# A second cross attention with its scores made twice, in rows and in columns, a norm moved between engines, and another order at the program's end

## The chip, the cores and the metric

The kernel runs on one core of one Trainium2 chip. The metric is the device time of one execution of the whole program, in microseconds, as the median of several executions. Engines are named as in the profile: PE is TensorE, PEld its weight loads, DVE VectorE, ACT ScalarE, POOL GpSimd, SP the engine that issues DMAs.

## The reference, cut to what matters

A decoder of two layers works on x of shape (16, 112, 256), with a context of shape (16, 375, 256). Each layer is self attention, cross attention over the context and a feed-forward part, and each of the six ends in a layer norm over x plus its result. The change touches the second layer: the cross attention (16 heads of 16 dimensions), the norm behind the coupled self attention ahead of it, and the end of the last part.

```python
q = x @ W_q + b_q
kv = memory @ W_kv + b_kv
scores = jnp.einsum('bhqd,bhkd->bhqk', q, k) * (1.0 / np.sqrt(HD))
scores = jnp.where(pad[:, None, None, :], -jnp.inf, scores)
A = jax.nn.softmax(scores, axis=-1)
ctx = jnp.einsum('bhqk,bhkd->bhqd', A, v)
...
x = _layernorm(x + y @ W_o + b_o, axis=-1)
```

## The kernel before, in words

The program is a row of stages (`stage_...` functions). Inside a stage every engine runs its own hand-written list of work, and semaphores (`then_inc`, `wait_ge`) tie the lists together. No planner moves anything: the order on an engine is the order in the source, and an engine that waits holds up all that is behind it on that engine. The helper `split_product` (lines 102 to 106) writes one exact product as three, of high and low parts, so its matmuls carry the lines 104, 105 and 106 in every stage.

`stage_cross_attention` serves both layers; the second call (`cross1`) is the one replaced. It loops over the 16 batches, and in a batch over 16 heads, with the batch after it prepared in between ("front": the context turned, C0 and C1; queries, Q; keys, K0 and K1; values, V0 to V2). Queries and keys are split in high and low parts, stored to DRAM and loaded back stacked (`stack`, lines 592 and 597), so that one product of 96 rows makes an exact score. For a head i of a batch, PE makes the scores in rows, 112 queries by 376 keys (line 730), DVE adds the mask, copies them out of PSUM and takes the maximum in one instruction (line 941), ACT makes exponentials (line 845), PE turns the probabilities three blocks at a time so that the keys lie on partitions (`turn`, line 738), ACT and DVE in turns copy them back to SBUF (lines 851 and 948), and PE multiplies them with the values, four heads at a time (line 751). Tables in each engine's list say at which head a front unit or a part of the tail runs:

```python
TAIL_AT = {6: 0, 8: 1, 10: 2, 15: 3}
FRONT_AT = {2: V0, 4: V1, 6: V2, 7: C0, 8: C1, 10: Q, 12: K0, 14: K1}
```

`stage_coupled_attention`, the stage before it, loops over the same batches with four groups of four heads. Its norm is made by DVE (`normalise`, line 1428) from y, a mean and POOL's power (`root`, line 1106); ACT has a list with two pairs of `tanh` (lines 1299 and 1304), the copy of the heads' columns (`copy_columns`, line 1330) behind them, and copies of turned probabilities (line 1324).

`stage_switch` is the last stage. Behind its 128 slots, eight "units" of gated outputs are left. For each, DVE multiplies by gates (`by_gates`, line 2692), ACT rounds the product (`high`, line 2602), POOL makes the low part (`low`, line 2421), and PE does twelve products (`outputs`, lines 104 to 106). Sums, statistics and norms of four chunks of four batches each (lines 2703 to 2724) stand between them on DVE.

## Time and profile before

| | us |
|---|---|
| median of 3 runs (lowest, highest) | 2426.97 (2423.71, 2427.23) |
| the profiled execution, its own time | 2411.24 |
| its span in the trace | 2409.5 |
| PE busy (share) | 2186.7 (91%) |
| DVE busy | 1728.6 (72%) |
| ACT busy | 1275.1 (53%) |
| POOL busy | 535.0 (22%) |

The shares are averages over all stages. What a change in one stage is worth is read from that stage: from the period of its loop, from what PE waits for in it, and from the rows in order of time. The second cross attention takes the time from about 1145 to 1519 us of the span, the coupled attention that from about 937 to 1143, and the last stage that from about 1532 to the end.

### The profile page before, as it was taken

Reading aid. Unit: us, or ns where it says so; the run is one execution under the profiler, and the core shown is the slowest. Engines: PE = TensorE matmul, PEld = TensorE weight load, DVE = VectorE, ACT = ScalarE, POOL = GpSimd, SP = SyncE. Lnnn points to the kernel's source line nnn. Section 1 sums busy time; section 2 is a strip of 40 time slices with the busy share of each in tenths; the row PEclk is TensorE's granted clock in tenths of the full one; section 3 lists DMA queues with packets and bytes.
Section 4 is the critical chain, followed back from the end, with each engine's and each line's share of the span. In section 5 each row is a group of like instructions: output and inputs, shape, how many; then the busy total and the mean of one; then the engine's idle time right before and its main releaser. Section 6 shows DMA issues by size and latency. Waiting matters only on the chain. (4 is left out here: it accounts for less than half of the span.)

```text
span 2409.5 us, 48067 instructions
## 1 busy us (share of the span) xinstructions
PE 2186.7 (91%) x15771; PEld 1847.9 (77%) x15771; DVE 1728.6 (72%) x4277; ACT 1275.1 (53%) x2676; POOL 535.0 (22%) x435
## 2 busy tenths in 40 slices
PE   7789999868999987897899998799999999999995
PEld 5578777757999965664787887678888888888884
DVE  2467877775888864776577777677777777767564
ACT  3257666754666634665566666444444444444441
POOL 3200000041111062332100000023333333333333
PEclk9889999988999998999899999899999999999998
DMA  4066666323766521000666664133232333222222
GB/s 117 4 149 135 131 129 131 81 74 104 235 207 213 172 66 35 0 0 0 149 131 128 132 142 109 56 97 92 93 99 87 112 89 102 88 94 93 71 76 69
DMA packets 201755, 246.50 MB, mean 102 GB/s; under 512 B 58481, under 2 KB 176706, under 8 KB 201602
## 3 DMA queue, kind: packets, MB, share of 16 engines
q1 hardware_dynamic: 198050, 235.37, 37.2%
q0 software_dynamic: 3552, 9.18, 1.3%
q8 instruction: 85, 1.39, 0.2%
q14 instruction: 68, 0.56, 0.1%
HBM read 202.95 MB, written 41.55 MB: 101 GB/s over the span
## 5 line engine op out<-in xcount | busy, mean ns | idle before, releaser
L845 ACT ACTIVATE cross_pr<-cross_sc,cross_mn 112x375 f32<-112x375 f32 x512 | 307.4, 607 | 222.8 <-DVE cross_mn L941 221.9
L2421 POOL TENSOR_TENSOR switch_gl<-switch_gb,switch_gh 128x896 fp32r<-128x896 f32 x128 | 270.7, 2116 | 574.8 <-ACT switch_gh L2602 574.8
L941 DVE CUSTOM_DVE_ANT_0 cross_sc<-cross_ps,cross_masked 112x375 f32<-112x375 f32 x512 | 271.6, 544 | 83.3 <-PE cross_ps L730 81.2
L738 PE MATMUL cross_ps<-all_ident,cross_pr 112*125 112x112 f32 x1536 | 255.7, 275 | 42.8 <-DVE cross_pt L948 41.9
L738 PEld LDWEIGHTS cross_ps<-all_ident,cross_pr 112*125 112x125 f32 x1536 | 232.5, 189 | 68.1 <-DVE cross_pt L948 38.9
L2658 DVE SCALAR_TENSOR_TENSOR switch_vt<-switch_ps,switch_chosen,switch_vt 112x128 f32<-112x128 f32 x512 | 144.1, 345 | 191.7 <-PE switch_ps L106 186.9
L730 PE MATMUL cross_ps<-cross_k,cross_q 96*112 96x376 f32 x512 | 212.8, 416 | 13.4 <-DMA cross_k<-cross_k_dram 11.6
L104 PE MATMUL switch_ps<-switch_vw,switchgates_xh 128*112 128x512 f32 x512 | 209.2, 408 | 4.9 <-ACT switch_vt L2581 4.9
L104 PE MATMUL switch_ps<-switch_gh,switch_ow 128*128 128x448 f32 x512 | 192.5, 376 | 18.6 <-POOL switch_gl L2421 17.3
L106 PE MATMUL switch_ps<-switch_vw,switchgates_xl 128*112 128x512 f32 x512 | 202.3, 395 | 0.0
L105 PE MATMUL switch_ps<-switch_vw,switchgates_xh 128*112 128x512 f32 x512 | 201.6, 394 | 0.0
L2581 ACT ACTIVATE switch_vt<-switch_ps,switch_chosen 112x128 f32<-112x128 f32 x512 | 145.9, 367 | 93.5 <-PE switch_ps L106 80.7
L105 PE MATMUL switch_ps<-switch_gl,switch_ow 128*128 128x448 f32 x512 | 190.6, 372 | 0.0
L106 PE MATMUL switch_ps<-switch_gh,switch_ow 128*128 128x448 f32 x512 | 190.4, 372 | 0.0
L2602 ACT CAST switch_gh<-switch_gb 128x896 fp32r<-128x896 f32 x128 | 121.7, 951 | 52.5 <-DVE switch_gb L2692 51.7
L672 POOL TENSOR_TENSOR cross_rstd<-cross_var,cross_half 112x1 f32<-112x1 f32 x32 | 17.3, 541 | 580.0 <-DVE cross_var L963 580.0
L2692 DVE TENSOR_TENSOR switch_gb<-switch_gb,switch_ct 128x896 f32<-128x896 f32 x128 | 138.6, 1084 | 0.0
L104 PE MATMUL experts_ps<-experts_xh,experts_w 128*128 128x256 f32 (+1 forms) x400 | 124.7, 312 | 6.4 <-ACT experts_h L1929 3.0
L948 DVE COPY cross_pt<-cross_ps 125x336 f32<-125x336 f32 x256 | 128.3, 501 | 1.6 <-PE cross_ps L738 1.5
L104 PEld LDWEIGHTS switch_ps<-switch_gh,switch_ow 128*128 128x128 f32 x512 | 98.2, 192 | 38.2 <-POOL switch_gl L2421 20.0
L730 PEld LDWEIGHTS cross_ps<-cross_k,cross_q 96*112 96x112 f32 x512 | 90.7, 178 | 43.1 <-issue 27.7
L1929 ACT ACTIVATE experts_h<-experts_ps,experts_b1c 128x256 f32<-128x256 f32 x168 | 79.9, 475 | 81.5 <-PE experts_ps L106 79.2
(399 smaller groups left out, 5656.2 us busy)
## 6 DMA issues: line engine op xcount, KB each, us to landing
switch_gb<-switch_gt_rows SPq DMA_DIRECT2D x128, 448.0 KB, 3.6
experts_w_raw<-in_L_ffn_w_dram SPq DMA_DIRECT2D x42, 1024.0 KB, 5.4
cross_k<-cross_k_dram SPq DMA_DIRECT2D x96, 375.0 KB, 8.0
cross_k_dram<-cross_ks SPq DMA_DIRECT2D x32, 750.0 KB, 4.7
all_place<-in_ctx_dram SPq DMA_DIRECT2D x32, 375.0 KB
cross_q<-cross_q_dram SPq DMA_DIRECT2D x192, 56.0 KB, 4.5
all_place<-in_L_ffn_v_w_dram SPq DMA_DIRECT2D x16, 512.0 KB, 6.2
all_place<-in_L_ffn_o_w_dram SPq DMA_DIRECT2D x8, 1024.0 KB, 7.4
```

What stands on the lines that cost most here:

```text
L104: nc.tensor.matmul(out, w[0], x[0], start=first, stop=False)
L105: nc.tensor.matmul(out, w[0], x[1], start=False, stop=False)
L106: return nc.tensor.matmul(out, w[1], x[0], start=False, stop=last)
L730: nc.tensor.matmul(ps[0:T, SCORES + h % 2, 0:KEYS], q[parity][:, h // 2, h % 2, :], kk[parity][:, h // 2, :], start=True, stop=True).then_ ...
L738: last = nc.tensor.transpose(ps[0:KP, TURNED + h % 2, t * T:(t + 1) * T], pr[:, h % NB, t * KP:(t + 1) * KP], ident[0:T, 0:T])
L845: nc.scalar.activation(pr[:, h % NB, :], sc[:, h % NB, :], ACT.Exp, bias=mn[parity][:, h:h + 1], scale=-1.0).then_inc(exped, 1)
L941: nc.vector.tensor_tensor_reduce(out=sc[:, h % NB, :], in0=ps[0:T, SCORES + h % 2, 0:S2], in1=mask_of[:], scale=-0.25, scalar=3e38, op0=AL ...
L948: nc.vector.tensor_copy(pt[:, h % NB, :], ps[0:KP, TURNED + h % 2, 0:KT * T]).then_inc(pt_dve, 1)
L2421: pool.tensor_tensor(gl[u % 2][:], gb[u % RING][:], gh[u % 2][:].bitcast(F32), ALU.subtract)\
L2581: last = nc.scalar.activation(vt[b % 2][:, e, :], ps[0:T, VALUES, e * PW:(e + 1) * PW], ACT.Copy, scale=chosen[h % 2][:, b, e:e + 1])
L2658: last = nc.vector.scalar_tensor_tensor(out=part, in0=ps[0:T, VALUES + 1, e * PW:(e + 1) * PW], scalar=chosen[h % 2][:, b, EH + e:EH + e + ...
L2692: nc.vector.tensor_tensor(gb[u % RING][:], gb[u % RING][:], ct[n % 2][:].unsqueeze(1).broadcast_to([P, EU, CT]), ALU.mult).then_inc(gated, 1)
```

## The change

**Second cross attention** (`stage_cross_columns`, in the place of the second call of `stage_cross_attention`). The scores are made twice. PE makes them in rows, as before (97 stacked rows: the mask is now a row of the stacked keys, made by POOL), and DVE only takes the maximum. When the maxima of eight heads are there, PE turns them, DVE splits minus the maxima in a high and a low part (`split_maxima`), and SP copies these by one DMA for each head and part, 16 for a half batch, into two more rows of the stacked queries (`stack_maxima`). PE then makes the scores again in columns, keys on partitions, four heads and 125 keys at a time (`columns`: two products of 256 columns), now with mask and minus maximum inside, and ACT makes exponentials of 448 elements a partition, straight into the tile that PE multiplies with the values. Turning the probabilities and copying them back (lines 738, 851 and 948) falls away. Three of a batch's twelve column units run in its own loop step, nine in the next; the tail lags two batches. Stacks are loaded by halves.

```diff
+        MASK_ROW, MAX_ROW, ROWS = 3 * PAIR, 3 * PAIR + 1, 3 * PAIR + 3
...
+        Q_PARTS, K_PARTS, M_PARTS = 6, 3, H
+        COLUMNS_OF_LAST = {1: 3, 2: 4, 3: 5, 5: 6, 6: 7, 7: 8, 9: 9, 10: 10, 11: 11}
+        COLUMNS_AT = {13: 0, 14: 1, 15: 2}
+        VALUES_AT = {1: 0, 5: 1, 9: 2, 13: 3}
+        HALF_OF_LAST_AT, HALF_AT = 1, 9
...
+            def stack_maxima(b, parity, part):
+                wait_apart(sp, sp_passed, (m_ready, b * HALVES + part + 1))
+                for n, bits in enumerate((mh, ml)):
+                    for h in range(H // 2):
+                        sp.dma_start(q[parity][MAX_ROW + n:MAX_ROW + n + 1, part * 4 + h // 2, h % 2, 0:T].bitcast(F32),
+                                     bits[part][h:h + 1, :].bitcast(F32)).then_inc(m_stacked[part], 16)
...
+                nc.tensor.matmul(ps[0:T, SCORES + h % 2, 0:KEYS], q[parity][0:MAX_ROW, h // 2, h % 2, 0:T],
+                                 kk[parity][0:MAX_ROW, h // 2, :], start=True, stop=True).then_inc(s_done, 1)
...
+            def turn_maxima(b, parity, part):
+                pe.wait_ge(s_max, b * H + (part + 1) * (H // 2))
+                nc.tensor.transpose(ps[0:H // 2, SCORES + 1, TURNED_AT:TURNED_AT + T],
+                                    mx[parity][:, part * (H // 2):(part + 1) * (H // 2)], ident[0:T, 0:T]).then_inc(m_turned, 1)
+
+            def columns(b, parity, n):
+
+                g, t = n // KT, n % KT
+                if n % (UNITS_OF_COLUMNS // 2) == 0:
+                    pe.wait_ge(m_stacked[2 * n // UNITS_OF_COLUMNS], (b + 1) * M_PARTS * 16)
+                wait(pe, exped, b * UNITS_OF_COLUMNS + n - 1)
+                for i in range(2):
+                    pair = 2 * g + i
+                    last = nc.tensor.matmul(ps[0:KP, COLUMNS + n % 2, i * 2 * QCOLS:(i + 1) * 2 * QCOLS],
+                                            kk[parity][:, pair, t * KP:(t + 1) * KP],
+                                            q[parity][:, pair].rearrange("r i t -> r (i t)"), start=True, stop=True)
+                last.then_inc(st_done, 1)
...
+                nc.scalar.activation(pt[:, n % RING], ps[0:KP, COLUMNS + n % 2, :].rearrange("p (a b) -> p a b", b=QCOLS)[:, :, 0:T],
+                                     ACT.Exp, scale=0.25).then_inc(exped, 1)
...
+                nc.vector.reduce_max(mx[parity][:, h:h + 1], ps[0:T, SCORES + h % 2, 0:S2], axis=AX.X).then_inc(s_max, 1)
...
+            def split_maxima(b, part):
+
+                wait_apart(dve, dve_passed, (m_turned, b * HALVES + part + 1), (m_stacked[part], b * M_PARTS * 16))
+                bank = ps[0:H // 2, SCORES + 1, TURNED_AT:TURNED_AT + T]
+                nc.vector.tensor_scalar_mul(mh[part][:], bank, -1.0).then_inc(m_high, 1)
+                wait_apart(dve, dve_passed, (m_high, b * HALVES + part + 1))
+                nc.vector.scalar_tensor_tensor(out=ml[part][:], in0=bank, scalar=-1.0, in1=mh[part][:].bitcast(F32),
+                                               op0=ALU.mult, op1=ALU.subtract).then_inc(m_ready, 1)
```

On SP, a step of the loop of the second cross attention before is this (two batches make one turn of the loop; `cross1_q1` and `cross1_k1` are the stacked queries and keys of odd batches).

```order
L576 DMA cross1_q_dram1<-cross1_qs 128x4x112
...
L580 DMA cross1_k_dram1<-cross1_ks 128x4x375
...
L564 DMA all_place1<-in_ctx_1024_dram 125x3x256
...
L569 DMA cross1_mask_raw0<-in_mask_BxS2_bf1_dram 112x375
...
L592 DMA cross1_q1<-cross1_q_dram1 16x8x112 x6
L597 DMA cross1_k1<-cross1_k_dram1 32x8x375 x3
```

And this is one step of it in the changed kernel (`cross1_mh` and `cross1_ml` are the high and low parts of minus the maxima).

```order
L1158 DMA cross1_q1<-cross1_mh1 1x16x7 x8
L1158 DMA cross1_q1<-cross1_ml1 1x16x7 x8
...
L1146 DMA cross1_q1<-cross1_q_dram1 16x4x112 x6
L1150 DMA cross1_k1<-cross1_k_dram1 32x4x375 x3
...
L1116 DMA all_place1<-in_ctx_1024_dram 125x3x256
...
L1121 DMA cross1_mask_raw0<-in_mask_BxS2_bf1_dram 1x375
...
L1158 DMA cross1_q0<-cross1_mh0 1x16x7 x8
L1158 DMA cross1_q0<-cross1_ml0 1x16x7 x8
...
L1146 DMA cross1_q1<-cross1_q_dram1 16x4x112 x6
L1150 DMA cross1_k1<-cross1_k_dram1 32x4x375 x3
...
L1127 DMA cross1_q_dram0<-cross1_qs 128x4x112
...
L1131 DMA cross1_k_dram0<-cross1_ks 128x4x375
```

A step has grown from 13 DMAs to 54: 32 rows of maxima, and the 9 loads of a stack are now 18 of half the size, with each batch of 16 rows between them.

On PE, this is what the changed kernel has from the turning of a batch's first eight maxima (line 1304) to the first of the column units that need them (the last row; line 1299 is a score in rows, 1315 a column unit, 1328 values, 1276 queries).

```order
L1304 MATMUL cross_ps<-all_ident,cross_mx 8x112
...
L1315 MATMUL cross_ps<-cross_q,cross_k 125x256 x2
L1354 MATMUL cross_ps<-all_ident,cross_xn 128x112 x2
...
L1328 MATMUL cross_ps<-cross_pt,cross_v 32x112 x12
...
L1299 MATMUL cross_ps<-cross_k,cross_q 112x376
L1315 MATMUL cross_ps<-cross_q,cross_k 125x256 x2
...
L1276 MATMUL cross_ps<-all_xt,all_place 128x112 x3
...
L1299 MATMUL cross_ps<-cross_k,cross_q 112x376
...
L1315 MATMUL cross_ps<-cross_q,cross_k 125x256 x2
```

Between the turn and that unit stand, in all, two other column units, one turned norm, one quad of values, four scores, the queries and the first half of the keys.

**Norm of the coupled attention.** POOL also makes minus mean times the root, and ACT, not DVE, makes the normed rows, ahead of its copy of group 2; DVE makes minus the mean; ACT's copy of the columns goes ahead of the tanh.

```diff
                 if before:
+                    copy_columns(b - 1)
                 if not last:
                     tanh(b + 1, 1 - parity)
...
+                if before == 2:
+                    normalise(b - 2)
                 evacuate(b, 2)
...
+                nc.scalar.activation(xn[:], y[:], ACT.Identity, bias=offset[:], scale=rstd[:]).then_inc(xn_ready, 1)
...
+                nc.vector.tensor_scalar_mul(minus_mean[:], mv[:, 0:1], -1.0)
```

**End of the last stage.** For the last eight units POOL makes the low part of one expert and DVE that of the other, and DVE's list behind slot 128 is written out by hand.

```diff
+                experts = slice(0, EU if u < SHARED else EU // 2)
+                pool.tensor_tensor(gl[u % 2][:, experts, :], gb[u % RING][:, experts, :],
+                                   gh[u % 2][:, experts, :].bitcast(F32), ALU.subtract).then_inc(low_ready, 1)
...
+                nc.vector.tensor_sub(gl[u % 2][:, 1, :], gb[u % RING][:, 1, :], gh[u % 2][:, 1, :].bitcast(F32))\
+                    .then_inc(low_dve, 1)
```

On DVE, before, from the gates of the sixth of the eight units on (2692 gates, 2703 sum, 2710 to 2719 statistics, 2724 norm):

```order
L2692 TENSOR_TENSOR switch_gb<-switch_gb,switch_ct 128x896
L2710 TENSOR_TENSOR all_x<-all_x,switch_ps 112x1024
L2714 BN_STATS switch_st<-all_x 112x6 x4
L2717 BN_AGGR switch_mv<-switch_st 112x2 x4
L2719 TENSOR_SCALAR switch_var<-switch_mv 112x4
L2724 TENSOR_SCALAR all_x<-all_x,switch_mv,switch_rstd 112x256 x4
L2692 TENSOR_TENSOR switch_gb<-switch_gb,switch_ct 128x896 x2
L2703 TENSOR_TENSOR switch_yt<-switch_ps,switch_yt 128x2x448
```

and in the changed kernel, from the gates of the seventh on (3273 gates, 3354 low part, 3284 sum, 3291 to 3300 statistics, 3305 norm):

```order
L3273 TENSOR_TENSOR switch_gb<-switch_gb,switch_ct 128x896
L3305 TENSOR_SCALAR all_x<-all_x,switch_mv,switch_rstd 112x256 x4
L3273 TENSOR_TENSOR switch_gb<-switch_gb,switch_ct 128x896
L3354 TENSOR_TENSOR switch_gl<-switch_gb,switch_gh 128x448
L3291 TENSOR_TENSOR all_x<-all_x,switch_ps 112x1024
L3295 BN_STATS switch_st<-all_x 112x6 x4
L3298 BN_AGGR switch_mv<-switch_st 112x2 x4
L3300 TENSOR_SCALAR switch_var<-switch_mv 112x4
L3354 TENSOR_TENSOR switch_gl<-switch_gb,switch_gh 128x448
```

The gates of the last two units now stand ahead of the statistics of the third chunk, not behind them.

## Rows read from the trace of the kernel before

**Rows 1.** Busy time by stretch: second cross attention's loop, then the program's end.
```profile
1168.80:1508.50 339.70, 315.47 (x3320) 271.89 (x3320) 269.48 (x888) 232.43 (x510) 21.29 (x44) 0.99 0.62 131
2346.00:2403.60 57.60, 33.30 (x147) 28.28 (x146) 32.85 (x73) 9.05 (x11) 22.11 (x12) 0.85 0.21 66
```
(Columns: stretch, its length, busy time of PE, PEld, DVE, ACT and POOL with counts, granted clock, DMA share, GB/s.)

**Rows 2.** PE in order of time, one batch: start, length, what, idle before.
```profile
1300.47 0.33 PE L730 MATMUL cross_ps<-cross_k,cross_q 96*112 96x376 f32 x1
1300.64 0.48 PE L738 MATMUL cross_ps<-all_ident,cross_pr 112*125 112x112 f32 x3
1300.88 0.41 PE L730 MATMUL cross_ps<-cross_k,cross_q 96*112 96x376 f32 x1
...
1301.38 0.36 PE L104 MATMUL cross_ps<-cross_w_high,cross_cx_high 128*125 128x256 f32 x1
...
1302.26 0.78 PE L751 MATMUL cross_ps<-cross_pt,cross_v 125*32 125x112 f32 x24
...
1309.13 1.06 PE L713 MATMUL cross_ps<-all_xt,all_place 128*128 x8
1310.20 1.12 PE L770 MATMUL cross_ps<-all_place,cross_o 128*112 128x256 f32 x4
1310.97 0.52 PE L730 MATMUL cross_ps<-cross_k,cross_q 96*112 96x376 f32 x1
...
1312.07 0.42 PE L104 MATMUL cross_ps<-cross_cx_high,cross_w_high 128*128 128x376 f32 x1
...
1313.28 0.78 PE L751 MATMUL cross_ps<-cross_pt,cross_v 125*32 125x112 f32 x24
1313.99 0.42 PE L730 MATMUL cross_ps<-cross_k,cross_q 96*112 96x376 f32 x1
1315.04 0.58 PE L738 MATMUL cross_ps<-all_ident,cross_pr 112*125 112x112 f32 x3 [0.63 <-DVE cross_pt L948]
...
1322.42 0.33 PE L730 MATMUL cross_ps<-cross_k,cross_q 96*112 96x376 f32 x1
```

**Rows 3.** Groups of PE instructions, 1200 to 1450 us: busy, mean ns, idle before.
```profile
L738 PE MATMUL cross_ps<-all_ident,cross_pr 112*125 112x112 f32 x543 | 90.3, 275 | 16.2 <-DVE cross_pt L948 16.2
```

**Rows 4.** Groups of DVE instructions, the same stretch.
```profile
L941 DVE CUSTOM_DVE_ANT_0 cross_sc<-cross_ps,cross_masked 112x375 f32<-112x375 f32 x182 | 96.6, 544 | 25.3 <-PE cross_ps L730 24.5
L926 DVE SCALAR_TENSOR_TENSOR cross_qs<-cross_ps,all_qk_bias,cross_qs 128x112 fp32r<-128x112 f32 x24 | 6.9, 328 | 0.0
```

**Rows 5.** SP in order of time: DMA issues (start, length for all xN).
```profile
493.71 0.25 SPq L1642 DMA_DIRECT2D experts_b_all<-in_L_ffn_bs_dram  x1
...
907.72 7.29 SPq L1080 DMA_DIRECT2D coupled_Jd<-in_L_attn_J_attn_dram  x16
...
1301.22 2.85 SPq L592 DMA_DIRECT2D cross_q<-cross_q_dram  x6
```

**Rows 6.** The page's list of DMA issues: KB each, median us to landing.
```profile
coupled_Jd<-in_L_attn_J_attn_dram SPq DMA_DIRECT2D x16, 1.0 KB, 1.5
```

**Rows 7.** PE alone by stretches of 3 us: busy, granted clock, DMA share, GB/s.
```profile
2349.00:2352.00 3.00, 0.51 (x3) 1.00 0.00 0
2352.00:2355.00 3.00, 3.00 (x11) 0.57 0.41 158
...
2361.00:2364.00 3.00, 0.21 (x2) 1.00 0.00 0
2364.00:2367.00 3.00, 2.74 (x12) 1.00 0.41 149
```

**Rows 8.** Coupled attention, all engines in order of time, one batch.
```profile
1061.63 0.53 ACT L1330 COPY coupled_osb<-coupled_ps 128x448 f32<-128x448 f32 x1
...
1062.21 0.65 PE L1208 MATMUL coupled_ps<-all_ident,coupled_osb 128*112 128x128 f32 x4 [1.29 <-ACT coupled_osb L1330]
...
1063.08 1.75 DVE L1428 TENSOR_SCALAR coupled_xn<-coupled_y,coupled_mv,coupled_rstd 112x256 f32<-112x256 f32 x1 [0.62 <-POOL coupled_rstd L1106]
```

**Rows 9.** The program's end, all engines in order of time.
```profile
2378.66 1.22 DVE L2710 TENSOR_TENSOR all_x<-all_x,switch_ps 112x1024 f32<-112x1024 f32 x1 [2.73 <-PE switch_ps L2528]
...
2383.14 2.09 DVE L2692 TENSOR_TENSOR switch_gb<-switch_gb,switch_ct 128x896 f32<-128x896 f32 x2
...
2385.27 4.13 POOL L2421 TENSOR_TENSOR switch_gl<-switch_gb,switch_gh 128x896 fp32r<-128x896 f32 x2 [2.01 <-ACT switch_gh L2602]
```

More of the change, by code:

```diff
@@ L1105, in root @@
                 pool.wait_ge(var_ready, b + 1)
-                pool.tensor_tensor(rstd[:], var[:], half[:], ALU.pow).then_inc(rstd_ready, 1)
+                pool.tensor_tensor(rstd[:], var[:], half[:], ALU.pow).then_inc(root_ready, 1)
+                pool.wait_ge(root_ready, b + 1)
+                pool.tensor_tensor(offset[:], minus_mean[:], rstd[:], ALU.mult).then_inc(rstd_ready, 1)
             def store(b):
@@ L1334, in copy_output, with normalise @@
                 nc.scalar.copy(o[:].rearrange("p a b -> p (a b)"), ps[:, TAIL, 0:DC * T]).then_inc(o_ready, 1)
+            def normalise(b):
+                act.wait_ge(rstd_ready, b + 1)
+                wait(act, x_stored, b)
+                nc.scalar.activation(xn[:], y[:], ACT.Identity, bias=offset[:], scale=rstd[:]).then_inc(xn_ready, 1)
             def copy_normed(b):
@@ L1349, in batch @@
                 exponent(b, 1)
+                if before:
+                    copy_columns(b - 1)
                 if not last:
                     tanh(b + 1, 1 - parity)
-                if before:
-                    copy_columns(b - 1)
                 evacuate(b, 1)
@@ L1358, in batch @@
                     turned_tanh(b + 1, 1 - parity)
+                if before == 2:
+                    normalise(b - 2)
                 evacuate(b, 2)
@@ L1417, in statistics @@
             def statistics(b, ch):
+                wait(dve, xn_ready, b)
                 ch.link(nc.vector.tensor_add(y[:].unsqueeze(1), x[:, ds(b, 1), :], o_bias[:].unsqueeze(1)))
@@ L1440, in batch @@
                 shift(b, 2, ch)
-                if before == 2:
-                    normalise(b - 2)
                 if before:
@@ L2386, in load_gates @@
                 wait(sp, low_ready, u - RING + 1)
+                wait(sp, low_dve, u - RING + 1 - SHARED)
                 sp.dma_start(gb[u % RING][:].rearrange("p e s -> p (e s)"),
@@ L2432, in _ @@
                     low(u)
-                c = turned_at(g)
-                if c is not None:
+                for c in ROOTS_BEHIND.get(u, ()):
                     root(c)
@@ L2505, in outputs @@
                 pe.wait_ge(low_ready, u + 1)
+                wait(pe, low_dve, u + 1 - SHARED)
                 if i == 0:
@@ L2736, in _ @@
             steps = iter(())
-            for g in range(END):
+            for g in range(SLOTS):
                 p, b = g // B, g % B
@@ L2767, in _, with low @@
                         nc.vector.tensor_sub(low_bits, raw, high_bits.bitcast(F32)).then_inc(ow_low, 1)
-                c = turned_at(g)
-                if c is not None:
-                    statistics(c)
-                    if c:
-                        normalise(c - 1)
-            normalise(NC - 1)
+            def low(u):
+                dve.wait_ge(high_ready, u + 1)
+                wait(dve, unit_done, u - 1)
+                nc.vector.tensor_sub(gl[u % 2][:, 1, :], gb[u % RING][:, 1, :], gh[u % 2][:, 1, :].bitcast(F32))\
+                    .then_inc(low_dve, 1)
+            last, u = HS * NC - 1, SHARED
+            attend(last, 0)
+            by_gates(u)
+            add_columns(last - 2)
+            by_gates(u + 1)
+            low(u)
+            attend(last, 1)
+            by_gates(u + 2)
+            low(u + 1)
+            statistics(0)
+            by_gates(u + 3)
+            low(u + 2)
+            low(u + 3)
+            statistics(1)
+            by_gates(u + 4)
+            low(u + 4)
+            by_gates(u + 5)
+            add_columns(last - 1)
+            low(u + 5)
+            by_gates(u + 6)
+            normalise(0)
+            by_gates(u + 7)
+            low(u + 6)
+            statistics(2)
+            low(u + 7)
+            normalise(1)
+            add_columns(last)
+            statistics(3)
+            normalise(2)
+            normalise(3)
 def stage_store(nc, x, out):
```

481 lines of the change are left out of this document (469 added, 12 removed).

## The prediction

> **What bounds the kernel now.** I read the busy time by stretch first. In the loop of the second cross attention PE is busy 315.47 of 339.7 us, DVE 269.48 and ACT 232.43 [rows 1]: PE sets the pace, DVE and ACT have some 20 to 30% to spare. The rows in order of time then show what PE does. From one batch's score at 1300.47 to the same one at 1322.42 is a period of 21.95 us, and starts are close behind each other, with one wait of 0.63 us for DVE's copy of turned probabilities at 1315.04 [rows 2]. The groups say how much of that there is: 16.2 us in 250 us before line 738 [rows 3], or 1.4 us in each of the 11.4 batches that such a stretch holds. What counts is therefore PE's list and whatever PE has to wait for. In the program's end the picture is another one: PE is busy for only 33.3 of 57.6 us [rows 1], in a chain of engines that wait for each other.
>
> **Second cross attention, PE's own work.** Removed: 16 turns of three blocks, each holding PE from 1300.64 to 1300.88, 0.24 us [rows 2], or 3.9 us a batch, and the 1.4 us of waits for their copies. Added: 24 products of 256 columns. The six such products of a value unit take from 1301.38 to 1302.26 [rows 2], 0.147 us each with the start of the group in it; a pair has more of the start, so I take 0.32 us for a column unit, 12 x 0.32 = 3.8 us. Two small turns of maxima at no more than a score's 0.2 us add 0.4 us. Net: -3.9 - 1.4 + 3.8 + 0.4 = **-1.1 us a batch**, 16 batches: -17.6 us. The scores in rows have 97 rows in place of 96 and cost what they did.
>
> DVE loses the copies of line 948 and the mask, ACT its copies of line 851, and ACT makes 12 longer exponentials instead of 16. All of it lies beside PE's work and I cost it at nothing: both engines had room before. It does not come back later, since PE stays the bound.
>
> **Second cross attention, the new wait.** The first column unit of each half batch waits for 16 rows of maxima, and these go one by one through SP's queue. Three pieces make the way from the turned maxima to that unit.
>
> - DVE takes a maximum, then the high and the low part. The nearest rows are 544 ns for the old maximum and 328 ns for a small two-operand instruction [rows 4]; with the high part at a little less, 0.5 + 0.3 + 0.3 = 1.1 us.
> - SP issues 16 DMAs. The nearest row is the load of the Jd blocks, 16 small DMAs of 16 pieces each, back to back: 7.29 us, or 0.455 us each [rows 5]. The six loads of queries in the loop take 0.475 us each, and the cheapest issue of a single row in the trace took 0.25 us, with a start 0.29 us ahead of the next [rows 5]. A row of maxima has 16 pieces like a Jd block, and so I take 0.455: 7.3 us. The bound from below is 16 x 0.29 = 4.6 us.
> - The last one lands. The Jd blocks landed in 1.5 us [rows 6]; I take that.
>
> Together 9.9 us. Meanwhile PE has this much to do, for the first half: two column units (0.64), a turned norm (0.4), a quad of values (1313.28 to 1313.99, 0.71), the queries (1309.13 to 1310.20, 1.07), keys (1312.07 to 1313.28, 1.21), and four scores of 0.25 with a last column unit at 0.32 [rows 2]: 5.4 us. For the second half it is three column units, one of them ahead of the values, the values, two value units of 0.88, the turned tokens (0.34), the output product (1310.20 to 1310.97, 0.77) and four scores: 5.4 us as well. So PE stands for 9.9 - 5.4 = **4.5 us, twice a batch**. There are 16 such waits for first halves and 15 for second ones inside the loop, 31 x 4.5 = +139.5 us. All of PE's list is behind the waiting unit, scores too, so nothing fills the gap.
>
> Is SP free when the rows come? In a batch it issues 54 DMAs in place of 13. 32 x 0.455 = 14.6 us, 12 loads of queries x 0.475 = 5.7 us and 6 of keys at about the same, 2.9 us, with four more (1.6 us) make 24.8 us. That alone is above the old period, and below the new one, 21.95 - 1.1 + 9.0 = 29.9 us. So it adds nothing by itself, but it also shows that the old pace is out of reach at this price.
>
> After waits this long the clock is in question. PE stood 4.09 us ahead of 2351.5, with 0.51 us of work in the 3 us around it, and in the 3 us after that the granted clock was 0.57, near the lower of its two levels (1.2 of 2.4 GHz); after a stretch with 0.21 us of work in 3 us it stayed at 1.00 [rows 7]. The new waits of 4.5 us are nearer to the first. A stretch of 3 us at 0.57 loses 1.3 us. I take 1.0 us for each wait, since not each will have it: 31 x 1.0 = +31 us. Bounds: 0, and 2.9 us if the low clock lasts for 5.8 us behind each wait.
>
> **Ends of that stage.** Behind the last score the eight last maxima go the whole way, 9.9 us, then six column units follow at the pace of ACT's exponential (about 0.7 us each), and a quad of values. Before, it was three turns and two quads of values, some 4.5 us. This is +10.7 us. At the start the stack is loaded only when the keys, too, are in DRAM, and by twice as many DMAs: +1.5 us.
>
> **Coupled attention.** DVE's norm took 1.75 us next to POOL's work and ACT's copy of the columns stood behind the tanh, which PE waited 1.29 us for in a batch of 13.2 us [rows 8]. But ACT's work ahead of PE's next tanh product is only put in another order, and the norm now stands in ACT's queue, behind the turned tanh that PE has to deliver first. I expect PE to win most of a wait and to find another: -0.2 us a batch, -3 us in all, between -16 (all of the 1.29 us goes) and +6 (the normed rows come 0.4 us later to PE in each batch).
>
> **The end.** POOL's low part was 2.07 us a unit, and twice it stood behind two sets of gates and two others of ACT and DVE [rows 9]. Halved, it is about 1.0 us, with DVE's half (0.55 us, half of one gate product) beside it, and the last two gates, which began at 2383.14, no longer stand behind the statistics that began at 2378.66 and the norm after them, 4.5 us [rows 9]. Of PE's 24 us without work there [rows 1], two waits behind a pair of gates go by some 4 us each and the others by 1 us for each unit left: 2 x 4 + 4 = 12 us. -12 us, between -6 (the shares of POOL and DVE exclude each other, as in [rows 8], where DVE's norm took 1.75 us beside POOL) and -16.
>
> **Sum.** 139.5 + 31 - 17.6 + 10.7 + 1.5 - 3 - 12 = +150 us. Against the profiled execution of 2411.2 us (span 2409.5) this is 2561 us; that execution is 15.8 us under the median of the runs shown, and I take the change against the median: 2427 + 150 = **2577 us**.
>
> **A rule of the skill.** The trace shows 7.29 us of issue for 16 DMAs that land 1.5 us after it [rows 5, 6]: the issue is the larger part. The Trainium skill (DMA: Bandwidth & Descriptors, Issuing engines are not separate DMA queues) says that the time a sequencer needs to initiate a DMA is usually small relative to the DMA itself. By that rule the 16 rows would hardly cost more than one, and the change would win; it is the first rival. The same page (Rules for kernel authors) says that many small transfers should be put together into one large one, which speaks against this change.
>
> **Rivals.**
>
> 1. *The rows of maxima arrive in time, and it is faster* (0.13). The mechanism: issues of one short row overlap so far that 16 of them and the landing take less than 5.4 - 1.1 = 4.3 us, under 0.18 us an issue. Then PE has no wait: -17.6 + 5 (end of stage) + 1.5 - 15 = -26 us, 2401 us. For it: the cheapest issue is half of the Jd price. Against it: even that one is 0.25 us [rows 5].
> 2. *The cheap issue price* (0.20). At 0.29 us the way is 1.1 + 4.6 + 1.5 = 7.2 us and the wait 1.8 us, too short for the clock: 31 x 1.8 = 56, - 17.6 + 8 + 1.5 - 15 = +33 us, 2460 us.
> 3. *PE goes cold at every wait* (0.17): 31 x 2.9 in place of 31, +59 us, 2636 us. The measured 4.09 us speaks for it, the 1.00 after the shorter pause against.
> 4. *It cancels* (0.05): waits of about 1 us eat what the turns gave, 31 x 1 - 17.6 + 6 + 1.5 - 15 = +6 us, about 2430 us.
>
> My forecast has 0.45. The sign turns at an issue price of about 0.23 us: there the waits are 0.8 us, and 31 of them cost what the rest gives.
>
> **How the numbers follow.** Slower: 0.45 + 0.20 + 0.17 = 0.82. Faster 0.13, same 0.05, within 0.2% (5 us), about what a measurement of this kernel can tell from no change. The range leaves out rivals 1 and 4, 0.18 together, and reaches from below the cheap price, 2440, to above the cold case, 2640. The slower cases have that range for their own.
>
> **What would show it.** In the loop: a period near 31 us; PE idle ahead of the first column unit of each half, put down to a DMA on the stacked queries, about 4.5 us each; SP's groups of 8 and 8 rows at about 7 us; no line for turned probabilities; DVE's and ACT's share far lower. In the end: 12 us less from the last slot to the last norm. I am wrong if the rows are issued in under 4 us, if PE's wait there is short, or if the period is SP's own sum and no wait stands at the columns.

## The result, and the profile after

The changed kernel takes 2720.92 us (median of 4 runs, 2717.97 to 2725.88), the kernel before 2426.74 us on the same chip: ratio 1.1217, 95% interval 1.1197 to 1.1238, or **294 us slower**. The forecast was slower by 150 us, 2577 us, with a range up to 2640 us. The direction was right, the size was half of what came, and the range missed it.

The busy time by engine, from the page of the changed kernel (engine, busy us, share of the span, instructions). PE's share fell from 91% to 82%, DVE's from 72% to 62%, ACT's from 53% to 44%.

```profile
PE 2230.5 (82%) x15419; PEld 1878.3 (69%) x15419; DVE 1676.1 (62%) x3965; ACT 1197.0 (44%) x2500; POOL 582.7 (21%) x473
```

Where the time went is read best between four instructions of PE that both kernels have: the first turn of the coupled attention's weights, its last turned norm, the first score of the second cross attention, and that stage's last turned norm. In order of time, before:

```profile
907.42 3.65 PE L1144 MATMUL coupled_ps<-all_ident,all_place 128*128 128x128 f32 x16 [3.91 <-PEq L49]
...
1142.95 0.61 PE L1230 MATMUL coupled_ps<-all_ident,coupled_xn 112*128 112x112 f32 x2 [2.57 <-issue]
...
1168.77 0.94 PE L730 MATMUL cross_ps<-cross_k,cross_q 96*112 96x376 f32 x2 [5.73 <-DMA cross_k<-cross_k_dram]
...
1518.20 0.63 PE L776 MATMUL cross_ps<-all_ident,cross_xn 112*128 112x112 f32 x2 [2.53 <-DVE cross_xn L967]
```

and in the changed kernel:

```profile
920.29 3.65 PE L1718 MATMUL coupled_ps<-all_ident,all_place 128*128 128x128 f32 x16 [3.90 <-PEq L49]
...
1150.32 0.61 PE L1804 MATMUL coupled_ps<-all_ident,coupled_xn 112*128 112x112 f32 x2 [3.09 <-issue]
...
1174.48 0.94 PE L1299 MATMUL cross_ps<-cross_k,cross_q 97*112 97x376 f32 x2 [7.24 <-DMA cross_k<-cross_k_dram]
...
1836.22 0.64 PE L1354 MATMUL cross_ps<-all_ident,cross_xn 112*128 112x112 f32 x2 [2.59 <-DVE cross_xn L1544]
```

| stretch | before | after | difference | forecast |
|---|---|---|---|---|
| start to coupled attention | 907.4 | 920.3 | +12.9 | 0 |
| coupled attention | 235.5 | 230.0 | -5.5 | -3 |
| to the first score | 25.8 | 24.2 | -1.7 | +1.5 |
| **second cross attention** | 349.4 | 661.7 | **+312.3** | +163.6 |
| last stage, to the end (spans 2409.5, 2717.1) | 891.3 | 880.9 | -10.4 | -12 |

The first line has nothing to do with the change (last section); without it the difference of the two profiled executions is 294.7 us, that of the medians. So all of the error lies in the second cross attention.

One half batch of it, all engines in order of time, changed kernel, with the PE rows between left out:

```profile
1472.30 0.26 PE L1304 MATMUL cross_ps<-all_ident,cross_mx 112*8 112x112 f32 x1
...
1472.59 0.54 DVE L1496 TENSOR_TENSOR cross_cx_low<-cross_ps,cross_cx_high 128x375 fp32r<-128x375 f32 x1
...
1473.05 0.54 DVE L1516 TENSOR_REDUCE cross_mx<-cross_ps 112x1 f32<-112x375 f32 x1
...
1473.50 0.25 DVE L1522 TENSOR_SCALAR cross_mh<-cross_ps 8x112 fp32r<-8x112 f32 x1
1473.90 0.26 DVE L1524 SCALAR_TENSOR_TENSOR cross_ml<-cross_ps,cross_mh 8x112 fp32r<-8x112 f32 x1 [0.15 <-DVE cross_mh L1522]
...
1474.27 4.95 SPq L1158 DMA_DIRECT2D cross_q<-cross_mh  x8
...
1476.65 0.33 PE L1299 MATMUL cross_ps<-cross_k,cross_q 97*112 97x376 f32 x1
...
1479.26 5.01 SPq L1158 DMA_DIRECT2D cross_q<-cross_ml  x8
...
1485.54 0.78 PE L1315 MATMUL cross_ps<-cross_q,cross_k 99*125 99x256 f32 x2 [8.56 <-DMA cross_q<-cross_ml]
```

This is the chain that the forecast drew, with other sizes. From the turn at 1472.30 to the column unit at 1485.54 it takes 13.24 us: 1.97 until the first row is issued, 10.00 for 16 issues (0.625 each), 1.27 for the landing. PE has work until 1476.98, for 4.7 us, then stands 8.56. This is a first half of a batch. In the second halves, by the mean of twelve batches, it is 2.48, 9.99 and 1.24 us, 13.7 in all, PE has work for 5.4 us and stands 8.35. Over the stage, what PE waited for (PE, line, released by: us in total, times, longest):

```profile
PE cross_ps L1315 <- DMA cross_q<-cross_ml: 279.0, 32, 20.4
PE cross_ps L1337 <- ACT cross_osb L1436: 7.2, 16, 0.7
```

The longest is the first wait, 20.4 us, the last was 6.0; the other 30 take (279.0 - 26.4) / 30 = **8.4 us each**. From the 5th to the 29th turn of maxima, twelve batches, the loop has a period of 39.9 us, where it was 21.95 [rows 2].

PE alone by stretches of 3 us around that half batch (busy, granted clock, DMA share, GB/s), with a reading as in [rows 7]:

```profile
1475.00:1478.00 3.00, 1.98 (x13) 1.00 0.28 89
1478.00:1481.00 3.00, 0.00 (x0) 1.00 0.02 1
1481.00:1484.00 3.00, 0.00 (x0) 0.63 0.02 1
1484.00:1487.00 3.00, 1.46 (x18) 0.50 0.16 30
1487.00:1490.00 3.00, 3.00 (x25) 0.50 0.66 162
1490.00:1493.00 3.00, 2.64 (x13) 0.67 0.58 135
```

The granted clock falls to 0.50, its lower level (1.2 GHz), during the wait, in which PE does nothing, and comes back some 6 us after PE has begun again. Over the twelve batches its mean is 0.75.

### The profile page after: what moved, and what is told of

The parts are those of the page before. It is cut to its first block and busy times, and to the rows that moved or that the text cites. A ratio compares the mean times of both kernels' runs of the same rounds, so it can differ in the third digit from the quotient of the medians.

```text
span 2717.1 us, 47322 instructions
## 1 busy us (share of the span) xinstructions
PE 2230.5 (82%) x15419; PEld 1878.3 (69%) x15419; DVE 1676.1 (62%) x3965; ACT 1197.0 (44%) x2500; POOL 582.7 (21%) x473
## 5 line engine op out<-in xcount | busy, mean ns | idle before, releaser
L3001 POOL TENSOR_TENSOR switch_gl<-switch_gb,switch_gh 128x896 fp32r<-128x896 f32 (+1 forms) x128 | 268.5, 2098 | 577.4 <-ACT switch_gh L3183 577.4
L1516 DVE TENSOR_REDUCE cross_mx<-cross_ps 112x1 f32<-112x375 f32 x256 | 138.8, 545 | 382.0 <-PE cross_ps L1299 380.1
L1315 PE MATMUL cross_ps<-cross_q,cross_k 99*125 99x256 f32 x384 | 106.8, 371 | 279.6 <-DMA cross_q<-cross_ml 279.0
L1429 ACT ACTIVATE cross_pt<-cross_ps 125x448 f32<-125x448 f32 x192 | 104.1, 545 | 457.4 <-PE cross_ps L1315 455.8
L1315 PEld LDWEIGHTS cross_ps<-cross_q,cross_k 99*125 99x125 f32 x384 | 88.4, 256 | 294.3 <-issue 211.7
L845 ACT ACTIVATE cross_pr<-cross_sc,cross_mn 112x375 f32<-112x375 f32 x256 | 153.9, 607 | 111.5 <-DVE cross_mn L941 111.3
L941 DVE CUSTOM_DVE_ANT_0 cross_sc<-cross_ps,cross_masked 112x375 f32<-112x375 f32 x256 | 135.8, 543 | 41.9 <-PE cross_ps L730 40.7
L738 PE MATMUL cross_ps<-all_ident,cross_pr 112*125 112x112 f32 x768 | 127.7, 275 | 21.5 <-DVE cross_pt L948 21.1
L738 PEld LDWEIGHTS cross_ps<-all_ident,cross_pr 112*125 112x125 f32 x768 | 116.3, 189 | 34.0 <-DVE cross_pt L948 19.5
L104 PE MATMUL experts_ps<-experts_hh,experts_w 128*128 128x256 f32 (+1 forms) x400 | 122.0, 305 | 1.3 <-issue 1.3
```

The lines of the kernel that those rows point to most:

```text
L104: nc.tensor.matmul(out, w[0], x[0], start=first, stop=False)
L738: last = nc.tensor.transpose(ps[0:KP, TURNED + h % 2, t * T:(t + 1) * T], pr[:, h % NB, t * KP:(t + 1) * KP], ident[0:T, 0:T])
L845: nc.scalar.activation(pr[:, h % NB, :], sc[:, h % NB, :], ACT.Exp, bias=mn[parity][:, h:h + 1], scale=-1.0).then_inc(exped, 1)
L941: nc.vector.tensor_tensor_reduce(out=sc[:, h % NB, :], in0=ps[0:T, SCORES + h % 2, 0:S2], in1=mask_of[:], scale=-0.25, scalar=3e38, op0=AL ...
L1315: last = nc.tensor.matmul(ps[0:KP, COLUMNS + n % 2, i * 2 * QCOLS:(i + 1) * 2 * QCOLS], kk[parity][:, pair, t * KP:(t + 1) * KP], q[parity ...
L1516: nc.vector.reduce_max(mx[parity][:, h:h + 1], ps[0:T, SCORES + h % 2, 0:S2], axis=AX.X).then_inc(s_max, 1)
```

## The experiments

The kernel before ran beside each group of kernels, on the same chip, and its time differs from group to group: its median was 2427.84 us beside r1 to r4, 2411.39 beside r5 to r8, 2423.85 beside r9 to r12 and 2410.44 beside r13 and r14. Below, "+120.6" is a median minus that of before on the same chip. The changed kernel is +294.2. All periods of loops below are those from the 5th to the 29th turn of maxima, twelve batches.

**r1: half of the rows.** The list `(mh, ml)` in `stack_maxima` is `(mh,)`.

> Left out: the eight rows with the low part of minus the maxima (they stay at one, their first value), so 8 row DMAs a half batch instead of 16. Theory A (the issues of the rows on SP, 0.625 us each, make PE's wait at the columns): SP's group shrinks by 8 x 0.625 = 5.0 us, so each of the 30 waits of 8.4 us becomes 3.4 us, and the first and the last shrink by 5.0 as well: 32 x 5.0 = 160 us less, and up to 30 x 2 = 60 us more if PE now keeps its clock: 2500 to 2560 us. Theory B (the wait ends with the landing or with the stacks, not with the issues): the waits hardly change, over 2680 us. Theory C (SP's sum of all its issues is the period): 32 x 5.0 us off SP's list as well, the same 2560 us, but then no wait of PE would be left at the columns.

(The rows of low parts stay at zero, not at one as that text says.) Measured: 2548.4 us, +120.6, ratio 1.0492 (1.0476 to 1.0508), 173.6 us less than the changed kernel. PE's wait and SP's group, in order of time:

```profile
1408.26 4.95 SPq L1158 DMA_DIRECT2D cross_q<-cross_mh  x8
...
1414.48 0.50 PE L1315 MATMUL cross_ps<-cross_q,cross_k 99*125 99x256 f32 x2 [3.54 <-DMA cross_q<-cross_mh]
```

Eight issues less, 5.0 us less of a wait: theory A holds. B falls with it, and C falls too, since a wait is left.

**r2: one DMA for eight rows.** The count `M_PARTS` is 2 to match.

```diff
-                    for h in range(H // 2):
-                        sp.dma_start(q[parity][MAX_ROW + n:MAX_ROW + n + 1, part * 4 + h // 2, h % 2, 0:T].bitcast(F32),
-                                     bits[part][h:h + 1, :].bitcast(F32)).then_inc(m_stacked[part], 16)
+                    sp.dma_start(q[parity][MAX_ROW + n:MAX_ROW + n + 1, part * 4:part * 4 + 4, :, 0:T].bitcast(F32),
+                                 bits[part][:].bitcast(F32)).then_inc(m_stacked[part], 16)
```

> The eight rows of a part go in one DMA (8 partitions of the small tile to one partition of the stack), so 2 DMAs a half batch instead of 16, with the whole computation kept. Theory A (issues make the wait): way = 1.9 (DVE) + 2 x 0.5 + 1.5 to 2.0 (landing) = 4.4 to 4.9 us against a cover of 4.7 us: waits of 0 to 0.4 us, no cold clock, so 2721 - 279 (all waits at the columns) - 30 to 60 (clock) = 2380 to 2410 us, below the kernel before. Theory B (a DMA of 8 pieces lands late, or its issue grows with its pieces): the wait stays over 3 us and the time over 2530 us.

Measured: 2418.68 us, -9.2, ratio 0.9961 (0.9947 to 0.9975): **a little faster than before**, and 303 us under the changed kernel.

```profile
1376.24 0.66 SPq L1157 DMA_DIRECT2D cross_q<-cross_mh  x1
1376.95 0.65 SPq L1157 DMA_DIRECT2D cross_q<-cross_ml  x1
...
1379.95 0.50 PE L1314 MATMUL cross_ps<-cross_q,cross_k 99*125 99x256 f32 x2 [1.07 <-DMA cross_q<-cross_ml]
```

A DMA of eight rows costs SP about what one row did. The loop's period is 20.5 us, 1.4 below that of before, so inside the loop the scores made twice do pay. Over the whole stage they do not: between the anchors above it takes 356.3 us, where before it took 349.4. The first wait at the columns is still 16.3 us, and from the last score (1517.45) to the last turned norm (1537.83) it takes 20.4 us, where before it took 11.5. The 9 us under before are those of the other two edits (r4, below, has 14). The 2380 to 2410 us expected had all the waits at the columns gone, and nothing lost at the end.

**r3 and r5: PE kept busy in the wait.** Ahead of each wait for the rows PE makes products into the free bank of columns, 56 in r3 and 32 in r5.

```diff
+                    wait(pe, exped, b * UNITS_OF_COLUMNS + n - 1)
+                    for f in range(32):
+                        nc.tensor.matmul(ps[:, COLUMNS + n % 2, 0:P], ident[:], ident[:], start=True, stop=True)
                     pe.wait_ge(m_stacked[2 * n // UNITS_OF_COLUMNS], (b + 1) * M_PARTS * 16)
```

> PE makes 56 extra products of 128 columns (0.13 us each at the high clock, 7.3 us) into the free column bank ahead of each of the two waits a batch, so that it doesn't stand. If the low clock behind a wait costs 2 us of PE's work each (PE's 21.9 us of work a period against some 18 at full clock): 2721 - 30 x 2 = 2660 us. If it costs 3 us each: 2630 us. If the low clock costs nothing on the path: 2721 us. All theories of the wait itself leave the columns waiting until the rows have landed.

Measured: 2775.79 us, +348.0, ratio 1.1437 (1.1419 to 1.1454). Inconclusive as a price: such a product is two instructions, and the filler took 12.7 us and outlasted the rows. But the granted clock is 1.00 over its whole loop, with a period of 43.2 us, so it gives PE's work at the full clock, and with that the next run.

> As r3_warm_filler, whose 56 extra products were two instructions each and took 12.66 us in place of 7.3 us. Now 32 products, 64 instructions of 0.113 us, 7.2 us, inside the wait of 8.4 us. In r3 a whole period's own work of PE, never cold, was 9.93 + 8.25 = 18.2 us, in the changed kernel it is 38.9 - 17.0 = 21.9 us: the low clock costs 3.7 us a batch, 1.85 us a wait. So 2721 - 30 x 1.85 = 2665 us, if that reading holds; 2721 us if the filler only fills and the clock isn't on the path; 2690 us if 1.0 us a wait, as forecast.

Measured: 2654.96 us, +243.6, ratio 1.101 (1.0993 to 1.1027), so 50.6 us less than the changed kernel's +294.2: more work on PE, and a shorter time. In order of time, then in stretches of 3 us:

```profile
1450.43 7.31 PE L1313 MATMUL cross_ps<-all_ident 128*128 128x128 f32 x64
...
1459.16 0.50 PE L1318 MATMUL cross_ps<-cross_q,cross_k 99*125 99x256 f32 x2 [1.42 <-DMA cross_q<-cross_ml]
```

```profile
1455.00:1458.00 3.00, 2.74 (x25) 1.00 0.02 1
1458.00:1461.00 3.00, 1.84 (x31) 1.00 0.21 38
1461.00:1464.00 3.00, 2.15 (x14) 1.00 0.75 162
```

The clock stays at 1.00 here, its mean over the loop is 0.98 where the changed kernel has 0.75, and the period is 36.4 us in place of 39.9. So filling a wait takes 1.7 us off it in the loop, and 50.6 / 32 = 1.6 us by the medians: the low clock costs at least that, since in r5 it is not quite always at 1.00. By PE's own work in r3 it is 2.35 us at most (worked out below). So it is neither the 1.0 that I took nor the 2.9 of the third rival.

**r4, r11, r12: the other two edits without the new cross attention.** r4 calls `stage_cross_attention` again for the second layer; r11 has of the rest the changed norm alone, r12 the changed end alone.

> The second cross attention of the kernel before, with the changed norm and the changed end. By the stages of the two traces: the coupled attention 5.5 us shorter, the end 10.4 us shorter, so 2427 - 16 = 2411 us. If these two are worth nothing by themselves: 2427 us. The forecast's terms gave -15.

> The kernel before with the changed norm of the coupled attention alone. The two traces gave 5.5 us for it (907.42 to 1142.95 before, 920.29 to 1150.32 after): 5.5 us below before. The forecast had 3, between 16 and -6.

> The kernel before with the changed end of the last stage alone. The two traces gave 10.4 us (from the last norm's turn to the end): 10 us below before, and with r11 together the 14.4 us of r4. The forecast had 12. If the gain of the end depends on the norm or the placing of code: r11 and r12 don't add up to 14.4.

Measured: r4 2413.48 us, -14.4, ratio 0.9942 (0.9929 to 0.9956); r11 2418.84 us, -5.0, ratio 0.9977 (0.9969 to 0.9986); r12 2414.75 us, -9.1, ratio 0.996 (0.9946 to 0.9975). They add up: -5.0 - 9.1 = -14.1. The new cross attention as written thus costs 294 + 14 = 309 us by itself.

**r6, r9, r10: can the new stage beat the old one?** All three are r2 with the first rows of maxima issued ahead of the second batch's stack, and the high row issued when it is ready. r6 also lets DVE split the maxima ahead of the first context unit, r9 does not, and r10 is r9 with PE's turn of the summed values moved behind the next batch's first score.

> r2 with three changes: the first rows of maxima are issued ahead of the second batch's stack; the row of high parts is issued when it is ready, not when the low ones are too; DVE splits the maxima ahead of the first context unit. In r2 the first wait at the columns was 16.28 us, and 15 waits of first halves 1.07 us each. If these are queue and order: -14 and -15 us, 2419 - 29 = 2390 us. If the first wait is only moved (the second batch's stack comes late in its place) and the short waits are the landing itself: 2410 to 2419 us.

Measured: 2395.43 us, -16.0, ratio 0.9933 (0.9919 to 0.9946).

> r6 without its change on DVE: the first context unit goes ahead of the split of the maxima again, as in r2. r6's loop had a period of 20.98 us against r2's 20.36, so theory: that reordering cost 0.6 us a batch (PE waits for the late low part of the context and the columns lose cover), and the rest of r6 (first rows ahead of the second stack, high parts issued early) is the gain. r6 stood 16.0 us below before on its chip; 15 x 0.6 = 9 us more: 25 us below before. If the period is set elsewhere: 16 us below before, as r6.

Measured: 2413.5 us, -10.4, ratio 0.9958 (0.9944 to 0.9972). **That theory fell**: r9's period is 20.98 us, r6's 20.67 and r2's 20.52, and r9 gains less on before than r6. I had read r6's period from a single batch.

> r9, and PE turns the summed values of a batch behind the first score of the next batch, not behind the last score of its own, where it stood 0.68 us a batch for ACT's copy. If that wait is on the path: 15 x 0.68 = 10 us below r9. If the wait only moves (to the columns, whose rows of maxima then come late by as much): as r9, within 3 us.

Measured: 2408.35 us, -15.5, ratio 0.9934 (0.9921 to 0.9947). Against r9 on the same chip 5 us less, but in the profiled executions the stage is no shorter (355.7 us between the anchors above, r9 355.9). r6 has 354.3, r2 356.3, and r4 with the old stage 349.3. r6, r10 and r4 lie within each other's intervals: all three beat before, and none beats the other two for certain. By the traces the new stage is in none of its forms shorter than the old one. In r2 the stretch from the first score to the last is only 2.0 us shorter than before (335.9 against 337.9), since the first wait and slow first batches take back what the loop gains, and the end is 8.9 us longer. In r6 the first wait is 8.2 us, half of r2's, yet its stage is 2.0 us shorter and no more.

**r7, r8, r13, r14: what is the price of an issue?** r8 issues the eight low rows on ACT's queue. r7 takes the high rows from a small tensor in DRAM, which goes as one piece of 112, where a row from SBUF is cut in 16 pieces of 7. r14 cuts r7's rows in 16 pieces too, and r13 makes the rows from SBUF 113 long, which go as one piece.

```diff
-                                     bits[part][h:h + 1, :].bitcast(F32)).then_inc(m_stacked[part], 16)
+                        source = m_dram[h:h + 1, :] if n == 0 else bits[part][h:h + 1, :].bitcast(F32)
```

> Left out: the high parts of minus the maxima; the eight rows are read from a small DRAM tensor with fixed numbers instead, 8 + 8 DMAs as in the changed kernel. If an issue from SBUF costs more than one from DRAM (0.625 against the 0.45 of the loads of queries, keys and Jd): the first group of 8 takes 3.6 us, the second 5.0 us, the wait shrinks by 1.4 us, 2721 - 32 x 1.4 = 2676 us. If the price belongs to the one destination row: both groups 5.0 us and 2721 us.

Measured: 2611.86 us, +200.5, ratio 1.0841 (1.0825 to 1.0858). SP's groups:

```profile
1402.97 2.31 SPq L1160 DMA_DIRECT2D cross_q<-cross_m_dram  x8
1405.33 4.93 SPq L1160 DMA_DIRECT2D cross_q<-cross_ml  x8
```

The group from DRAM is 2.7 us shorter than the other, more than either case had allowed for, and the waits fall with it, to 5.8 us (median).

> The eight low rows of a half batch are issued on ACT's queue, the eight high ones on SP's, at the same time. If the 0.625 us is each issuing engine's own time: the way is 2.0 + 5.0 + 1.3 = 8.3 us, the waits 3.6 us, 2721 - 32 x 4.9 - some clock = 2500 to 2565 us (r1: 2548). If both share one limit (the DMA engines or rings): 10 us of issues still, 2721 us or more, as ACT's exponentials now wait too.

Measured: 2581.74 us, +170.4, ratio 1.0713 (1.0697 to 1.073). In order of time:

```profile
1423.91 5.02 ACTq L1447 DMA_DIRECT2D cross_q<-cross_ml  x8
```

```profile
1423.98 5.24 SPq L1157 DMA_DIRECT2D cross_q<-cross_mh  x8
```

Both engines issue eight rows in 5 us at the same time, so 0.62 us is the issuing engine's own time, and no limit that both share. The first halves' waits fell to 80.1 / 16 = 5.0 us, not to the 3.6 expected: in one batch ACT begins its rows at 1440.70 and SP at 1439.56, since ACT's other work stands ahead of them. In the second halves PE stood some 4.3 us each for ACT's copy of the turned tokens, which was late behind ACT's issues. That is why r8 is not r1.

> The rows of maxima are 113 elements long in place of 112 (the last one is a zero that nobody reads), so each of the 16 DMAs from SBUF goes as one piece in place of 16 pieces of 7 elements; the whole computation is kept. Theory P (the issue price grows with the pieces into which a row is cut): 0.29 us a row as in r7's DRAM rows, 16 rows in 4.6 us, way 2.0 + 4.6 + 1.3 = 7.9 us, wait 3.2 us, about 115 to 125 us above before (r1 was 121). Theory S (a source in SBUF is what costs): 0.62 us a row as before, 294 us above before.

Measured: 2677.6 us, +267.2, ratio 1.1116 (1.1101 to 1.1132).

```profile
1414.45 4.71 SPq L1158 DMA_DIRECT2D cross_q<-cross_mh  x8
1419.20 4.64 SPq L1158 DMA_DIRECT2D cross_q<-cross_ml  x8
```

> As r7 (the eight high rows come from a small DRAM tensor with fixed numbers, high parts left out), but each of these rows is cut in 16 pieces of 7 elements, as the rows from SBUF are. Theory P (pieces): the group takes 5.0 us like the low rows', and the time is 294 us above before. Theory S (source): 2.3 us, and 200 us above before, as r7. Between them, as the 0.455 us of the Jd blocks, also 16 pieces from DRAM: 3.6 us and some 245 us above before.

Measured: 2706.11 us, +295.7, ratio 1.1237 (1.1218 to 1.1256).

```profile
1401.70 4.93 SPq L1161 DMA_DIRECT2D cross_q<-cross_m_dram  x8
1406.67 5.01 SPq L1161 DMA_DIRECT2D cross_q<-cross_ml  x8
```

r13 stands 27 us under the 294 of theory S and far above the 115 to 125 of P; r14 stands at the 294 of P and far from the 200 of S. From the start of one group to the start of the next, one row costs:

| | one piece | 16 pieces |
|---|---|---|
| from DRAM | 0.29 us (r7) | 0.62 us (r14) |
| from SBUF | 0.59 us (r13) | 0.62 us (changed kernel) |

So neither theory holds alone: either of the two, a source in SBUF or a cut in 16 pieces, takes a row from 0.29 to about 0.6 us, and both together add almost nothing. Why, no run tells. That pieces alone don't set the price is seen beside it: the loads of queries, 64 pieces of 112, still take 2.67 / 6 = 0.45 us in the changed kernel too.

## Why the prediction was right in direction and wrong in size

**The mechanism was right.** A wait stands ahead of the first column unit of each half batch, released by the low rows of maxima; SP's single issues make it; nothing fills it; r1 moves it by just what it takes off SP, and r2 and r8 by most of that. By the same runs the first rival (rows in time), the second (0.29 us an issue) and the fourth fall.

**The step that failed is "SP issues 16 DMAs ... 0.455 us each".** I took the price from the nearest-looking row, the Jd blocks, which come from DRAM and go to 16 partitions [rows 5]. Measured: 0.625 us, 9.99 us for 16 in place of 7.3. The upper bound was missing: I set one from below, 0.29, and none from above, though the trace of before had no row from SBUF to SBUF at all. The 0.29 was there too, in r7: a single piece from DRAM.

Its neighbours added to it. The turn to the first issue took 1.97 us in the first halves, not 1.1: DVE stood at a context unit's low part (1472.59) and a maximum (1473.05), ahead of the split in its list, and I had costed the three instructions without that queue. In the second halves it took 2.5. PE's cover, the work that it has meanwhile, was 4.7 us in the first halves, not 5.4: the queries took 0.81 us where I had 1.07, the keys 1.03 for 1.21, and the three column units 0.80 for 0.96. In the second halves the cover was 5.4 as I had it (by my own terms 5.5). So a wait is 13.24 - 4.7 = 8.5 or 13.7 - 5.4 = 8.4 us in place of 9.9 - 5.4 = 4.5: a difference of two near numbers, in which an error of 3.3 us on a way of 9.9 us is three quarters of the result. Over 30 waits this is 30 x 3.9 = +117 us of the 149 missed in the stage, and 2.7 us of each 3.9 are the issue price.

**The first wait, 20.4 us, was not in the list.** That is 16 us more than 4.5. SP in order of time at the stage's start, changed kernel:

```profile
1190.05 2.71 SPq L1146 DMA_DIRECT2D cross_q<-cross_q_dram  x6
1192.80 1.38 SPq L1150 DMA_DIRECT2D cross_k<-cross_k_dram  x3
...
1195.61 2.24 SPq L1121 DMA_DIRECT2D cross_mask_raw<-in_mask_BxS_bf_dram  x1
1197.88 5.34 SPq L1158 DMA_DIRECT2D cross_q<-cross_mh  x8
```

The first maxima were turned at 1184.00, but their rows stand in SP's list behind the second batch's stack, two contexts and a mask. I had asked whether SP is free in the loop, and not at the start. r6, with the first rows ahead of that stack, has 8.2 us there, where r2 has 16.3.

**The end of the stage.** From the last score to the last turned norm it takes 31.3 us (1804.90 to 1836.22), before 11.5 us: +19.8 where I had +10.7. The way of the last maxima gives 2.7 us of the 9.1 missed (12.57 us from 1807.06 to 1819.63, for 9.9). Behind it the clock is low again, and the changed kernel takes 16.6 us to the last turned norm where r2, which has the full clock for a part of it, takes 14.3. The rest of the 9.1 was not separated. With the 16 and the 117 us this makes 142 of the 149; the rest is spread over the batches.

**The clock and PE's own work were both off, and nearly cancelled.** With the clock at 1.00 throughout (r3) the period less the 12.4 us from each filler's start to its column unit leaves 43.2 - 2 x 12.4 = 18.4 us of PE's own work, 3.6 less than the period before, where I had 1.1 less. Queries and keys got cheaper beside the turns that went (above), and a column unit takes 0.29 us in the mean, not 0.32; the rest was not separated. In the changed kernel PE's own work is 39.9 - 2 x 8.4 = 23.1 us, so the low clock adds 4.7, or 2.35 a wait, where I had 2.0 and 1.0. Together +1.1 a batch against my +0.9. That these two cancel is luck: a right sum of two wrong terms would have looked like a confirmation, and only r3 and r5 separate them. The net price in r5 is 1.7 us a wait, smaller than 4.7 / 2: r5's clock is not quite full, and its two waits, filler included, are 0.2 to 0.3 us longer than those of the changed kernel. The 5.8 us of low clock behind a wait that bounded my price had no row under it; in the half batch above it is 6 to 7 us.

**SP's sum** did not bound, as forecast: 32 x 0.625 + 9.4 for the other 22 DMAs = 29.4 us a batch against a period of 39.9. (The period named as a sign, near 31, was itself short of my terms: 21.95 - 1.1 + 9.0 + 2.0 is 31.9.)

**The norm:** -5 us (r11) for -3. PE's waits in the coupled attention, before (the total for the copy that I had as 1.29 us a batch), then after:

```profile
PE coupled_ps L1208 <- ACT coupled_osb L1330: 18.4, 14, 1.6
```

```profile
PE coupled_ps L1804 <- ACT coupled_xn L1913: 8.8, 14, 2.7
PE coupled_ps L1782 <- DVE coupled_var L2008: 7.6, 14, 0.6
```

18.4 us of waits became 16.4, a new one for ACT's norm as foreseen. That is 2.0 us of the stage's 5.5; the rest these waits do not account for.

**The end of the program:** -9 to -10 us for -12, but not by the way that I gave. PE's waits in its last 60 us, before, then after:

```profile
PE switch_ps L104 <- POOL switch_gl L2421: 15.8, 5, 5.5
```

```profile
PE switch_ps L104 <- DVE switch_yt L3284: 5.1, 1, 5.1
PE switch_ps L104 <- POOL switch_gl L3001: 4.5, 1, 4.5
```

POOL's halved low part did not take 1.0 us. By the groups of that stretch (busy, mean ns, idle before):

```profile
L3001 POOL TENSOR_TENSOR switch_gl<-switch_gb,switch_gh 128x448 fp32r<-128x448 f32 x8 | 14.2, 1773 | 19.8 <-ACT switch_gh L3183 19.8
```

That is 1.77 us in the mean for half of what took 2.07. The eight differ by what DVE does at the time: 1.16 us twice, beside DVE's statistics; 1.57 to 1.60 four times, where DVE's own half (0.58) starts with it; 2.48 and 3.05 beside gates and probabilities. This is the bound that I had named and not taken. The trace shows that the length goes with DVE's work, and no run took that work away. Five waits for POOL, 15.8 us, became one of 4.5 us and one of 5.1 us for DVE's sum: 6.2 us less, where I had 12. What of the gain is the halves' and what the order's was not separated.

**Range and chances.** 0.82 for slower stood on the mechanism, and that held. The range was too narrow above: 2640 came from the cold clock alone. An upper bound for the issue at twice the 0.29 would have given a wait of 6.5 us, 62 us more over 31 waits, and with the cold clock an end of the range near 2700 us: nearer, and still not enough without the queues ahead of the links.

## What to carry to other kernels

Count DMAs, not bytes, when a chain goes through a queue: sixteen rows of 448 bytes a half batch, issued one by one, cost 303 us against the same bytes in two DMAs. A wait forecast as way minus cover carries the errors of both, so bound each from both sides and put the queue ahead of every link (DVE's list, SP's list at the stage's start) into the way. And a wait that lets PE's clock fall costs more than its length: here at least 1.6 us on top of 8.4. Last, read a stage from end to end: r2's loop was 1.4 us a batch under before, and its stage was 7 us longer.

## What the runs showed of the hardware that I had not expected

The issue price of one short row depends on more than its being one: 0.29 us from DRAM in one piece, 0.59 to 0.62 us in the three other cases (r7, r13, r14). A DMA of eight rows from eight partitions to one took SP 0.66 us, as one row did (r2). The Trainium skill (DMA: Bandwidth & Descriptors, Issuing engines are not separate DMA queues) says that the time to initiate a DMA is usually small relative to the DMA itself. Here one issue took 0.62 us and the last row landed 1.27 us after its issue, and sixteen issues in line took 10.0 us, so for rows this short the measurement says otherwise.

Some executions have a pause of PE in the experts stage that no semaphore explains, in code that the change does not touch. In the changed kernel:

```profile
877.79 0.74 PE L104 MATMUL experts_ps<-experts_xh,experts_w 128*128 128x448 f32 x1 [10.35 <-issue]
```

The profiles of r1 to r4 and r9 to r12 have pauses at the same place, of 4 to 11 us, in part put down to ACT; those of r5 to r8, of r13 and r14, and the profiled execution of before do not. The first are those beside which before had medians of 2424 to 2428 us, the second those with 2410 and 2411 us. It is not the chip alone: r5 to r8 and r9 to r12 ran on the same one. What it is stays open.
